# Queries and keys replicated through device memory instead of by selection matmuls, and expert weights split beside the first attention units

## What is computed

```python
def xattn(x, ctx):                       # x: (16, 256, 128), ctx: (16, 64, 128)
    q, k, v = (heads(y @ W.T) for y, W in ((layernorm(x), Wq), (ctx, Wk), (ctx, Wv)))
    scores = einsum('bhqd,bhkd->bhqk', q, k) / sqrt(8)
    attn = softmax(scores, axis=1)       # over the 16 heads
    return merge(einsum('bhqk,bhkd->bhqd', attn, v)) @ Wo.T

x = x + xattn(x, ctx)
y = layernorm(x)
routing = sigmoid(y @ centroids.T)       # top 2 of 8 experts, softmax of their two scores
x = x + y + sum over 2 shared experts + weighted sum over 2 routed experts
# an expert: gelu(y @ Wfc.T) @ Wproj.T with 512 hidden numbers
```

## Time and profile before

| | us |
|---|---|
| median of 3 runs | 528.89 (527.93 to 542.43) |
| the profiled execution | 525.64 |
| its span | 523.8 |
| first scores of attention start at | 53.36 |

### The profile page before, as it was taken

The page is one execution under the profiler, slowest core; times in us unless marked ns, Lnnn a source line. Parts: engine busy times, 40 slices in busy tenths (PEclk is TensorE's granted clock), DMA queues, the critical chain, the costliest instruction groups (busy, mean ns, idle before and its releaser), DMA issues.

```text
span 523.8 us, 11740 instructions
## 1 busy us (share of the span) xinstructions
PE 356.3 (68%) x3844; PEld 255.5 (49%) x3845; DVE 327.1 (62%) x639; ACT 279.5 (53%) x523; POOL 286.9 (55%) x293
## 2 busy tenths in 40 slices
PE   5786477768675766469602589969788888888700
PEld 2342244445453643156302357658677777777600
DVE  7994579999999596128104685455554554565437
ACT  3977533477776533158302358845654564465336
POOL 7598765687878427710771700515555655655610
PEclk9999659898988679569855889999999999999955
DMA  8900000000000001100110111032222222221057
GB/s 307 324 13 5 2 11 12 11 11 11 12 1 0 1 11 48 50 16 2 50 53 18 42 51 43 26 87 62 60 67 68 65 63 56 71 66 55 23 201 281
DMA packets 34250, 30.89 MB, mean 59 GB/s; under 512 B 13460, under 2 KB 30487, under 8 KB 33824
## 3 DMA queue, kind: packets, MB, share of 16 engines
q1 hardware_dynamic: 29664, 21.89, 14.0%
q0 software_dynamic: 4544, 8.44, 4.8%
HBM read 17.55 MB, written 12.62 MB: 58 GB/s over the span
## 4 chain that ended last, share of the span: by engine, by line
PE 39%; DVE 22%; issue 11%; ACT 10%; another core or an unknown queue 8%; POOL 5%; DMA 3%; ACTq 1%; SPq 0%; DVEq 0%; POOLq 0%
PE banks L1455 5%; DVE Mx L853 4%; ACT E L716 3%; PE banks L1468 3%; PE banks L1467 3%; POOL E L400 2%; PE banks L1255 2%; PE banks L1384 2%; DVE E L1143 2%; PE banks L1388 2%; PE banks L1386 2%; PE banks L1469 2%; ACT kRep L714 2%; PE banks L1453 2%
## 5 line engine op out<-in xcount | busy, mean ns | idle before, releaser
L479 POOL DMA_INDIRECT results<-E,qRep x78 | 83.4, 1069 | 75.3 <-DVE E L1135 52.5
L469 POOL DMA_INDIRECT gathered<-xs,slot x64 | 64.7, 1010 | 99.3 <-DVE xs L1021 54.3
L714 ACT ACTIVATE kRep<-banks 128x512 f32<-128x512 f32 x78 | 47.8, 613 | 68.3 <-PE banks L1455 66.6
L676 ACT ACTIVATE kRep<-banks 128x512 f32<-128x512 f32 x64 | 38.6, 603 | 82.3 <-PE banks L1370 37.9
L400 POOL TENSOR_TENSOR E<-E,rZ 128x1024 f32<-128x1024 f32 x32 | 68.3, 2157 | 24.6 <-DVE rZ L861 24.6
L1384 PE MATMUL banks<-wprojL,E 128*128 128x128 f16 x256 | 51.1, 231 | 40.2 <-DVE E L926 35.6
L1143 DVE TENSOR_TENSOR E<-kRep,E 128x512 f16<-128x512 f32 x78 | 53.9, 691 | 24.4 <-ACT E L716 16.6
L1467 PE MATMUL banks<-wprojL,E 128*128 x312 | 59.5, 219 | 11.4 <-DVE E L1143 9.5
L926 DVE TENSOR_TENSOR E<-kRep,E 128x512 f16<-128x512 f32 x64 | 43.6, 691 | 37.6 <-ACT E L677 32.4
L1468 PE MATMUL banks<-wprojH,E 128*128 x312 | 58.2, 218 | 3.0 <-issue 2.6
L1469 PE MATMUL banks<-wprojH,E 128*128 x312 | 58.2, 218 | 2.2 <-issue 2.2
(11 more groups left out here) (203 smaller groups left out, 932.1 us busy)
## 6 DMA issues: line engine op xcount, KB each, us to landing
qRep<-gathered SPq DMA_DIRECT2D x39, 129.0 KB, 1.9
qRep<-results SPq DMA_DIRECT2D x8, 512.0 KB, 6.7
E<-in_wfc_t SPq DMA_DIRECT2D x1, 2560.0 KB, 13.6
X<-in_x SPq DMA_DIRECT2D x4, 512.0 KB, 6.5
kPad<-kRep SPq DMA_DIRECT2D x128, 8.0 KB
out<-X SPq DMA_DIRECT2D x8, 256.0 KB, 3.8
xs<-in_wproj_t SPq DMA_DIRECT2D x1, 1280.0 KB, 14.2
results<-E,qRep POOLq DMA_INDIRECT x78
```

The source lines that it names most:

```text
L469: g.indirect_dma_start(out=gathered, out_offset=bass.IndirectOffsetOnAxis(ap=slot[:, k, i:i + 1], axis=0), in_=xs[:, i, :], in_offset=None ...
L479: g.indirect_dma_start(out=results, out_offset=bass.IndirectOffsetOnAxis(ap=xg[:, k, h, 2 * D:ROW].bitcast(I32), axis=0), in_=yg[:, k, h, ...
```

## The change

The selection matmuls are gone, with `select`, `kRep` and their evacuations. Instead the halves of k and q are written to two arrays in device memory (`k_rows`, `q_rows`) and read back in the replicated layout by DMA. Wk and Wq are first reordered on DVE (`rows_first`) so that a row of the product is what a partition needs. All of it is issued by SP, in an order written out by hand. ACT does the high halves of all four steps of q ahead of the first exponentials, and a high half waits until the stores of the step before, which read the same buffer, have landed.

The expert weights are loaded by eight DMAs that POOL issues. They are in four parts (`WEIGHT_PARTS`): 6 blocks and 4 of Wfc, 6 and 4 of Wproj. The parts of 6 are scaled within the copy on ACT and subtracted on DVE (`lows`); those of 4 are scaled and subtracted on POOL. Two blocks of the first part are split in the preamble, the rest on ACT, DVE and POOL between the first units.

```diff
-PROJ_PARTS = ((0, 1), (1, 6), (6, NE))
+WEIGHT_PARTS = ((0, 6), (6, NE), (0, 6), (6, NE))
-PAD_PARTS = 4 * QUARTER
+PAD_PARTS = 2 * QUARTER
...
+        hid = sb("hid", [P, FC, BANK])
+        q_rows = nc.dram_tensor("q_rows", (PAIRS, QUARTER, 2, DK, QUARTER, 2 * S), F16, kind="Internal").ap()
+        k_rows = nc.dram_tensor("k_rows", (2, QUARTER, DK, HH, PAIRS * SK), F16, kind="Internal").ap()
...
-            def pad_k(pair):
+            def pad_k(pair, quarters=(0, 1, 2, 3)):
                 j = pair % 2
                 if pair > 1:
                     sp.wait_ge(raw_ready, 2 * pair - 2)
...
+                for quarter in quarters:
+                    b, odd = divmod(quarter, 2)
+                    for low in range(2):
+                        r = 64 * low + 32 * b + 16 * odd
+                        src = k_rows[low, quarter].rearrange("d g (a s) -> d g a s", s=SK)[:, :, pair]
+                        sp.dma_start(kPad[r:r + 16, j, odd, :, b], src.unsqueeze(0).broadcast_to([2, DK, HH, SK])
+                                     ).then_inc(kPad_loaded[j], 16)
+            def store_q(n):
+                for low, done in enumerate((qhi_ready, qlo_ready)):
+                    for j in range(2):
+                        sp.wait_ge(done, 2 * n + j + 1)
+                        sp.dma_start(q_rows[2 * n + j, :, low].rearrange("b d g n -> b (d g) n"), qs[:, j, low]
+                                     ).then_inc(q_stored[j], 16)
+            def load_q(n):
+                for j in range(2):
+                    pair = 2 * n + j
+                    sp.wait_ge(q_stored[j], 32 * n + 32)
+                    src = q_rows[pair].rearrange("b l d g n -> (b l d) (g n)")
+                    for i in range(2):
+                        sp.dma_start(qRep[64 * i:64 * i + 64, pair].rearrange("p g q -> p (g q)"), src
+                                     ).then_inc(q_loaded[pair], 16)
...
+            pad_k(0, (0, 1))
+            store_q(0)
+            pad_k(0, (2, 3))
+            load_q(0)
+            store_q(1)
+            pad_k(1)
+            load_q(1)
+            store_q(2)
+            pad_k(2)
+            load_q(2)
+            store_q(3)
...
+            def scaled(part):
+                pool.wait_ge(weights_loaded[part], 32)
+                for e in range(4):
+                    w = raw_w[part][:, e]
+                    g.tensor_tensor(w, w, consts[:, 2, 0:1].broadcast_to([P, F]), ALU.mult).then_inc(weight_scaled, 1)
+            scaled(1)
+            scaled(3)
+            low_parts(1, 0)
+            low_parts(3, 4)
...
                     if again:
-                        act.wait_ge(spread[0], 2 * n + j + 1)
-                        act.wait_ge(spread[1], 2 * n + j + 1)
+                        act.wait_ge(q_stored[j], 32 * n)
                     s.activation(qs[:, j, 0], q_ps[j], ACT.Copy).then_inc(qhi_ready, 1)
...
+                    if first and k == 0:
+                        highs(1, 0, 4)
+                        spread_v(0, 0)
+                    if first and k == 1:
+                        highs(3, 0, 4)
+                        spread_v(1, 1)
+                    if first and k == 2:
+                        highs(2, 0, 6)
...
+                    if first and k == 0:
+                        lows(0, 2, 6)
...
+                    if first and k > 1:
+                        lows(2, 3 * k - 6, 3 * k - 3)
```

More of the change, by code:

```diff
@@ L290, in _ @@
-            for pair in range(PAIRS):
+                for quarter in quarters:
[5 more added lines that the diff above has]
+                                     ).then_inc(kPad_loaded[j], 16)
@@ L291, in _ @@
+            load_q(1)
[3 more added lines that the diff above has]
+            store_q(3)
+            pad_k(3)
+            load_q(3)
+            for pair in range(4, PAIRS):
                 pad_k(pair)
@@ L539, in copy_xnT @@
+                for i in range(TP):
+                    at = slice((2 * n + 1) * TP + i, (2 * n + 1) * TP + i + 1)
+                    last = s.activation(xn[:, 1, i], X[:, 2 * n + 1, i // 2, i % 2, :], ACT.Identity,
+                                        bias=shift[:, at], scale=rstd[:, at])
+                last.then_inc(xn1_ready, 1)
             def copy_xnT(n):
@@ L1219, in spread_parts @@
-            def spread_parts(i, which, high, low, reused):
-                for side in range(2):
-                    if reused:
-                        pe.wait_ge(spread_out[side], i)
-                    for g in range(2):
-                        sel = 2 * side + g
-                        t.matmul(spread_ps[side][:, g, :], select[:, which, 0, sel], high, start=True, stop=False)
-                        last = t.matmul(spread_ps[side][:, g, :], select[:, which, 1, sel], low, start=False,
-                                        stop=True)
-                    last.then_inc(spread[side], 1)
@@ L1243, in _, with project_q @@
[L1243 to L1247 removed]
+            def project_q(n, j, again):
+                pe.wait_ge(xnT_ready, 2 * n + j + 1)
+                if again:
+                    pe.wait_ge(qlo_ready, 2 * n + j - 1)
+                for half in range(2):
+                    for b in range(2):
+                        last = t.matmul(q_ps[j][64 * b:64 * b + 64, S * half:S * half + S],
+                                        wqP[:, 64 * half:64 * half + 64], xnT[:, j, S * b:S * b + S],
+                                        start=True, stop=True)
+                last.then_inc(q_ready, 1)
@@ L1331, in _ @@
             four_units(1)
+            pe.wait_ge(qlo_ready, PAIRS)
             for n in range(2, PAIRS // 2):
```

311 lines of the change are left out of this document (129 added, 182 removed).

## The result

| | before | changed |
|---|---|---|
| median of 4 runs each, us | 529.66 (527.93 to 542.43) | 551.33 (549.44 to 554.25) |
| ratio | | 1.0444 (95% interval 1.0401 to 1.0486) |
| first maximum of attention starts | 54.45 | 66.97 |
| last maximum of attention starts | 157.23 | 181.77 |

The change costs 21.7 us by the medians, about 23 by the ratio, which leaves out the one slow run of before (542.43). The forecast was 546.0, slower.

The account below looks back on a forecast made before the run. The chain to the first scores, then DVE, was taken to bound the kernel. 13.9 + 5.2 = 19.1 us gave 544.7 from the profiled run, 548 by the median; forecast 546, range 536 to 558 (0.60).

Parts of the forecast that it names:

- The narrow transfers: Preamble: q stores and key pads run on few DMA engines, whose work of 55.3 us from 12.2 paces the first unit.
- I take 4 and 2 engines: Preamble DMA: a store of q uses 4 engines and a pad 2, the same ones each time, by outermost count.
- Rival 1: Preamble: transfers spread over all engines, first unit's end 11.6 us earlier than before, total 522.5 or 517; chance 0.18.
- Term 1: Preamble: first attention unit's exponentials end at 75.2 instead of 61.27, held by stores, pads and loads; +13.9 us.
- the packet of a pad: Preamble pads: each 128-byte packet costs 14 ns of an engine, so pads of two pairs take 14.4 us.
- SP's issues fit beside it (0.69 each): Preamble: SP's issues, 0.69 us each, fit beside the work of the busiest DMA engine.
- Term 2: First attention units, up to unit 4's maximum: weights' split delays POOL's normalisation and adds DVE work; +5.2 us, ends 0 and 8.
- POOL's first normalisation later by 5 us: First units: POOL's four subtractions precede its first normalisation, 5 us later; unit 3's scores start 3.1 us late.
- Three low halves of wproj (0.7 each, as L786): DVE, between unit 2's sum and unit 4's maximum: three low halves add 2.1 us where DVE is the bound.
- And the three ahead of the maximum of unit 3 a wait too: DVE ahead of unit 3's maximum: three low halves only fill a wait for scores.
- The later pads cost nothing: During attention: later pads, 7.2 us a pair on two engines against 11.7 us per pair of attention, cost nothing.
- Nothing behind attention changes: After attention: no change in time is expected.

Follow-up runs that it names:

- e1: Changed kernel with the arrays in memory laid out so that stores of q and pads use 16 engines, rows of k stored twice: 539.17 us, ratio 1.0246.
- e8: Changed kernel with the pads of pairs 1 and 2 issued on SP behind the last stores of q: 550.36 us, ratio 1.0344.
- e4: Changed kernel without DVE's six low halves of wproj between the first units, POOL writing zeros there: 543.15 us, ratio 1.0332.
- e12: Against e10: POOL issues the third and fourth weight parts behind its scaling of the second; 443.77 us beside 443.62 for before, ratio 0.9999.
- e10: Against e6: first q stores ahead of the keys' wait, weight copies one step later, pads of pairs 1 and 2 late; 526.75 us, ratio 0.991; again 438.09, 0.9867.
- e6: Changed kernel with transfers on 16 engines and the whole weights' split in the preamble's waits: 530.35 us beside 531.57 for before, ratio 0.998.

## Why the prediction was right, and where a term was not

**The narrow transfers: right.** "I take 4 and 2 engines" is borne out by the 130 packets of a pad and by three levels of GB/s 27, 96 and about 240. e1 shows that it is the cause. Rival 1, spread over all engines, was the other reading of the earlier trace rows. When e1 made that come true, its price turned out to be wrong: the exponentials of unit 0 end at 60.26, 1.0 us ahead of before and not 11.6. Of the 10.6 us that are missing, some 6 are SP standing idle until the keys' stores were seen, 14.5 us after the first was issued beside the weights. My sum had let weights and small transfers follow one another at their bytes' price (1.5 us for the keys); where the rest lies was not worked out.

**Term 1: +13.9 forecast, +11.25 measured** (at the first maximum 12.5; 1.3 come back because the table load that stood between it and the exponentials is done ahead). The step as the prediction put it is stores 6, pads 7.2, loads 3: 16.2 us, against 14.84. By the levels of GB/s: stores 512 KB at 96 are 5.5; pads 128 KB at 27 are 4.8 (e8: 4.6); loads 1 MB at about 240 are 4.4. Sum 14.7. The mis-sized part is the packet of a pad. I took 14 ns from the earlier trace rows; at 27 GB/s on two engines it is 9.5 ns when they follow one another closely. The 6.1% over 4160 packets from 110 to 165 us give 12.9 ns by the same working as in the earlier trace rows. So the busy time that I had used as a price is more than the spacing at which such packets follow each other. The loads were priced too low by 1.4 us a step.

**"SP's issues fit beside it (0.69 each)": wrong, and without effect on the sum.** Pads held SP up to 4 us in one issue, but for the same reason for which the store was late: the two engines. The chain of waits books this time on SP (L284), which alone would lead one to remove issues; e1 issued more (four stores of k for one) and lost every hold.

**Term 2: +5.2 forecast, +11.4 measured** by the marks of the prediction: against before, the exponentials of unit 0 end 11.25 us later and the maximum of unit 4 starts 22.6 later (105.50 against 82.88). Unit 5 adds another 1.3. Its first part, POOL's first normalisation later by 5 us, is borne out: it starts 11.9 us after the exponentials of unit 0 (forecast 11.7), and e4, which keeps that and drops the lows, is 3.4 us late by the same marks (forecast 3.1).

The other 7.9 are the low halves, and two steps failed there. "Three low halves of wproj (0.7 each, as L786)", 2.1 us ahead of unit 4, took 5.68 on DVE and cost 5.4 (from the maximum of unit 3 to that of unit 4 it is 11.3 us, in e4 5.9). L786 reads one operand from PSUM; the low halves of the weights read both from SBUF, and POOL's normalisation does too, so that five of the six waited 2.0 us each for a POOL instruction. "And the three ahead of the maximum of unit 3 a wait too" held for 0.6 us each, not for 2.6: they took 7.66 us, and the wait covered all but 2.6.

**"The later pads cost nothing": right.** From unit 5 to unit 15 the shift against before grows by 0.6 us. **"Nothing behind attention changes": right in the medians** (21.7 and 23.2 us against 24.5); the one profile of the changed kernel ended 28.6 later, which its own run, the slowest of four, carries alone.

The total came out near by luck: term 1 was 2.7 us too high and term 2 6.2 too low, and of the 24.5 us by which the last maximum is late the medians show 21.7.

## What to carry to other kernels

Look at the outermost count of both sides of every new transfer before anything else: stores on four engines ran at 96 GB/s and loads at about 240, pads on two engines waited behind the stores and held the engine that issued them, and a chain of store, load and store again pays that several times. Bulk loads beside such a chain delay it: a store landed in 10 to 12 us in place of 4. Take a duration for a DVE instruction from one with the same operands in the same memories, and look what POOL runs in that moment: two SBUF operands on both made one wait for the other's whole instruction. Copies that have to be made somewhere belong in the waits that the change opens, not behind the point where an engine becomes the bound; that alone gave back 10 us here.

## What the runs showed that was not expected

- SP can be held inside the issue of a small transfer: 589/728/4074 ns (least, median, most) for pads on two engines, 598/599/627 when the same bytes went to 16.
- A store of 128 KB on all 16 engines landed in 3.7 us (e1, median of the preamble), in 11.9 (e12) with 2.5 MB of another queue in flight.
- The same kernel before took 528 to 532 us on some chips and 443.7 on others, with a mean granted clock of 0.86 to 0.88 and of 0.90 to 0.92. Up to the end of attention little differs: e10's first maxima start at 49.43 and 49.35, and from first to last it is 100.2 and 102.1 us. The profile of before has waits behind attention that it puts down to another core or an unknown queue, the longest in its chain (200 to 350 us):

```profile
251.55 30.31 another core or an unknown queue
```

All ten profiles from the slower chips have such a wait (30 us in nine, 18.5 in e6), none of the four from the faster chips has any. In before they are 8% of the span, 42 us, so about half of the 85 us between the chips. What they are was not tried. They do not decide the sign: the changed kernel is slower and e10 faster on both.
